# Routed feed-forward of a decoder: products over 512 tokens with transposed hidden rows, routing placed beside the groups, the loop over the chosen rows placed inside the last group

## What is computed

```python
xf = layernorm(x).reshape(-1, dim)                 # 4096 x 512
scores = softmax(xf @ w_gate.T)                    # 4096 x 8
s = (scores + expert_bias).reshape(N, 4, 2)
keep = the two groups of experts with the largest sums
topk_idx = top 2 of the kept experts               # 4096 x 2, values 0..7
weights = scores at topk_idx
counts = bincount(topk_idx)                        # rows of each run
routed_in = xf[topk_idx.reshape(-1)] * weights     # only xf[0..7] is ever gathered
h = silu(grouped(routed_in, w1, counts)) * grouped(routed_in, w3, counts)
out = (silu(xf @ sw1.T) * (xf @ sw3.T)) @ sw2.T
out = out.at[topk_idx.reshape(-1)].add(grouped(h, w2, counts))   # only rows 0..7 receive
result = x + out
```

## Time and profile before

| | |
|---|---|
| median of 3 runs | 2175.28 us (2170.5 to 2177.55) |
| the profiled execution: its own time | 2176.23 us |
| the profiled execution: its span | 2174.5 us |
| instructions | 47396 |
| TensorE matmul busy, share of the span | 2055.2 us, 95% |
| VectorE / ScalarE / GpSimd busy | 1304.4 us, 60% / 1056.6 us, 49% / 784.0 us, 36% |

### The profile page before, as it was taken

The page is one execution under the profiler, slowest core; times in us unless marked ns, Lnnn a source line. Parts: engine busy times, 40 slices in busy tenths (PEclk is TensorE's granted clock), DMA queues, the critical chain, the costliest instruction groups (busy, mean ns, idle before and its releaser), DMA issues. The chain is left out here.

```text
span 2174.5 us, 47396 instructions
## 1 busy us (share of the span) xinstructions
PE 2055.2 (95%) x14972; PEld 1579.0 (73%) x14972; DVE 1304.4 (60%) x3836; ACT 1056.6 (49%) x2763; POOL 784.0 (36%) x1435
## 2 busy tenths in 40 slices
PE   5999999999998999999979999999999699999886
PEld 4888888888885444445467888888888588888744
DVE  4777777777766677777746565555565333333354
ACT  3777676776776444444434445454544222212134
POOL 2455445545557466565522121212121111121100
PEclk8999999999999999999989999999999899999999
DMA  5121211311243121224121121111211562222100
GB/s 181 65 100 57 104 63 56 111 56 61 104 153 133 45 68 62 72 66 152 55 89 40 41 69 49 58 60 49 69 39 40 191 211 84 75 77 82 54 1 0
DMA packets 99823, 170.98 MB, mean 79 GB/s; under 512 B 12016, under 2 KB 22256, under 8 KB 99712
## 3 DMA queue, kind: packets, MB, share of 16 engines
q1 hardware_dynamic: 99712, 169.68, 23.0%
HBM read 136.08 MB, written 33.57 MB: 78 GB/s over the span
## 5 line engine op out<-in xcount | busy, mean ns | idle before, releaser
L489 POOL TENSOR_SCALAR a_probs<-a_probs,a_rinv 128x256 f32<-128x256 f32 x512 | 237.5, 482 | 283.9 <-DVE a_rinv L790 283.9
L597 ACT ACTIVATE a_probs<-a_probs,a_negm 128x256 f32<-128x256 f32 x512 | 254.6, 502 | 116.9 <-DVE a_negm L774 116.2
L489 POOL TENSOR_SCALAR c_probs<-c_probs,c_rinv 128x256 f32<-128x256 f32 x128 | 67.1, 534 | 394.6 <-DVE c_rinv L790 394.6
L774 DVE CUSTOM_DVE_ANT_0 a_probs<-bank,a_mbias 128x256 f32<-128x256 f32 x512 | 191.7, 417 | 6.3 <-PE bank L1033 4.6
L1439 ACT ACTIVATE b_gate<-bank,b_xs 128x512 f32<-128x512 f32 x128 | 87.9, 688 | 182.0 <-PE bank L1639 162.7
L783 DVE COPY a_pT<-bank 128x512 f32<-128x512 f32 x128 | 88.3, 690 | 141.8 <-PE bank L1050 141.6
L597 ACT ACTIVATE c_probs<-c_probs,c_negm 128x256 f32<-128x256 f32 x256 | 127.4, 502 | 90.0 <-DVE c_negm L774 90.0
L1050 PE MATMUL bank<-a_ident,a_probs 128*128 128x128 f32 x1024 | 155.9, 275 | 14.0 <-POOL a_probs L489 7.1
L1050 PEld LDWEIGHTS bank<-a_ident,a_probs 128*128 128x128 f32 x1024 | 122.6, 142 | 31.6 <-issue 10.4
L1639 PE MATMUL bank<-b_wg,b_xqT 128*128 128x512 bf16 x512 | 133.1, 383 | 2.3 <-DVE b_wu L1492 1.6
L1546 DVE SCALAR_TENSOR_TENSOR b_hid<-bank,b_xs,b_gate 128x512 f32<-128x512 f32 x128 | 95.9, 750 | 64.6 <-PE bank L1639 32.7
(11 more groups left out here) (289 smaller groups left out, 4786.6 us busy)
## 6 DMA issues: line engine op xcount, KB each, us to landing
m_ew<-in_L_ffn_w_dram SPq DMA_DIRECT2D x24, 512.0 KB, 8.4
a_cbuf<-in_ctx_dram SPq DMA_DIRECT2D x16, 512.0 KB, 6.9
a_xbuf<-in_x_dram SPq DMA_DIRECT2D x16, 512.0 KB, 6.4
a_resb<-in_x_dram SPq DMA_DIRECT2D x16, 512.0 KB, 3.6
x<-a_resb SPq DMA_DIRECT2D x16, 512.0 KB, 2.8
b_xbuf<-x SPq DMA_DIRECT2D x32, 256.0 KB, 2.7
b_resb<-x SPq DMA_DIRECT2D x32, 256.0 KB, 2.7
x<-b_resb SPq DMA_DIRECT2D x32, 256.0 KB, 2.0
```

What stands on the lines that cost most here:

```text
L489: last = nc.gpsimd.tensor_scalar(pr, pr, rinv[:, s, r:r + 1], 0.0, ALU.mult, ALU.add)
L597: nc.scalar.activation(pr, pr, ACT.Exp, bias=negm[:, s, h % 2, t:t + 1], scale=-1.0, accum_out=ssum[:, s, QT * (h % 2) + t:QT * (h % 2) + ...
L774: nc.vector.tensor_tensor_reduce(out=probs[:, s, h % 2, t], in0=s_bank[h][:, t * SEQ:(t + 1) * SEQ], in1=mbias[:, el.par], scale=-sm_scale ...
```

## The change

`routed_ffn_phase` is written anew; tensors are placed by hand in SBUF, and the eight banks of PSUM are shared by name. What it does:

1. 8 groups of 512 tokens take the place of 32 tiles of 128. In `gate` and `up` the weights are now the stationary operand and 512 tokens of turned rows the moving one, so the hidden rows come out already transposed, 128 features at a time. `turn_h` is gone. Each piece of hidden rows is split by ScalarE (HI, `hi_h`) and GpSimd (LO, `lo_h`), from SBUF.
2. `down` of group g stands in group g+1, one of its four tiles behind each `up`.
3. The logits are made transposed, with fp32r products of 512 columns (4 with HI and LO of the gate weights side by side, 4 more with LO of the rows), copied, and turned by 4 small transposes.
4. The routing is done per group (`route`), on VectorE, between `hidden` and `rows_out` of feature block 1 and `hidden` of feature block 2; ScalarE's Exp stands beside Silu in each group. What needs all counts (`runs`) stands behind group 6.
5. The table is made in two halves (w1 behind group 0, w3 behind group 1), with four experts side by side in strips of 32 columns, from expert weights that are loaded in two passes.
6. The loop over chosen rows has 16 steps of 512 rows. Its steps stand in "slots" between the halves (6 matmuls) of the last group's products. The scaled rows are split: GpSimd makes HI (`rows_hi`), VectorE makes LO (`rows_lo`), and `add_up` is one fp32r product of 512 columns (HI and LO side by side).
7. There is no second block and no barrier between stages.

The core of the diff (the `iteration` with `gate` and `slot` is TensorE's, the one that begins with `lo_x` VectorE's; `rows_lo` is VectorE's, `rows_hi` and `lo_h` are GpSimd's):

```diff
-                        def turn_h(el):
-                            pe.wait_ge(h_done, el.n + 1)
-                            wait_for(pe, th_lo, el.n)
-                            turn(th_bank, hid[:, el.par], th_done)
...
+        def gate(g, f, ks):
+            if ks[0] == 0:
+                if f == 0:
+                    pe.wait_ge(tx_lo, g.n * TILES + TILES)
+                wait_for(pe, silu_done, g.n * KC + f)
+            product(g_bank, lambda a, b, k: (sw[0][:, b, k, f * P:(f + 1) * P], xnT[:, g.par, a, k]), ks, g_done)
...
+    LOOP_FROM = 4
+    END_TURN, END_DOWN, END_FOLD = 23, 25, 28
+    def last_order():
+        units = [(u, f) for f in range(KC) for u in ("gate", "up", "down before")] + [("down", t) for t in range(TILES)]
+        halves = [(u, f, half) for u, f in units for half in range(2)]
+        for i, (u, f, half) in enumerate(halves):
+            yield u, f, half
+            if LOOP_FROM - 2 <= i < LOOP_FROM + STEPS + 2:
+                yield "slot", i - LOOP_FROM, 0
+            if i in (END_TURN, END_DOWN, END_FOLD):
+                yield "end", (END_TURN, END_DOWN, END_FOLD).index(i), 0
...
+        def iteration(g):
+            every = range(KC)
+            if number(g) == LAST:
...
+                        if is_step(i - 2):
+                            add_up(i - 2)
+                        if is_step(i + 1):
+                            turn_onehot(i + 1)
+                        if is_step(i):
+                            pick(i)
...
+            for f in range(KC):
+                gate(g, f, every)
+                if f == 0:
+                    turn_x(g.plus(1))
+                elif f == 1:
+                    logits_turned(g.plus(1))
+                up(g, f, every)
+                if f == 1:
+                    logits(g.plus(1))
+                if has_before(g):
+                    down(g.plus(-1), f, every)
+            if number(g) in (0, 1):
+                expert_rows(number(g))
...
+            for t in range(TILES):
+                lo_x(g.plus(1), t)
+            for f in range(KC):
+                hidden(g, f)
+                if has_before(g):
+                    rows_out(g.plus(-1), f)
+                if f == 0 and g.has(2):
+                    row_stats(g.plus(2))
+                if f == 1:
+                    route(g.plus(1))
...
+        def rows_lo(i):
+            for j in range(4):
+                dve.wait_ge(hrow_hi, 4 * i + j + 1)
+                V.scalar_tensor_tensor(hrow[:, i % 2, j, HID:2 * HID], act_a[:, i % 2, j],
+                                       weight[:, 2 * i + j // 2, j % 2:j % 2 + 1], hrow[:, i % 2, j, 0:HID].bitcast(F32),
+                                       ALU.mult, ALU.subtract).then_inc(hrow_lo, 1)
...
+        def rows_hi(i):
+            wait_for(pool, sum_done, i - 1)
+            for j in range(4):
+                wait_apart(pool, asilu_done, 4 * i + j + 1)
+                nc.gpsimd.tensor_scalar(hrow[:, i % 2, j, 0:HID], act_a[:, i % 2, j],
+                                        weight[:, 2 * i + j // 2, j % 2:j % 2 + 1], 0.0, ALU.mult, ALU.add).then_inc(hrow_hi, 1)
+        def lo_h(g, f):
+            wait_apart(pool, h_hi, g.n * KC + f + 1)
+            nc.gpsimd.tensor_tensor(hidT[:, g.par, LO, f], hid[:, f % 2], hidT[:, g.par, HI, f].bitcast(F32),
+                                    ALU.subtract).then_inc(h_lo, 1)
```

More of the change, by code:

```diff
@@ L1697, in ternary_ffn_phase, with routed_ffn_phase @@
     return phase
-def routed_ffn_phase(nc, tag, x_in, out, w_gate, w1, w2, w3, sw1, sw2, sw3, expert_bias, spent=(), tiles=TOK // P):
+def routed_ffn_phase(nc, ctx, banks, tag, x_in, out, w_gate, w1, w2, w3, sw1, sw2, sw3, expert_bias, tiles=TOK // P):
     EXPERTS, HID = w1.shape[0], w1.shape[2]
@@ new lines, in routed_ffn_phase, with sb, sem, row_of_smalls @@
+    TILES = 4
+    WIDE = TILES * P
+    groups = tiles // TILES
+    LAST = groups - 1
+    STEPS = tiles // 2
+    def sb(name, at, shape, dt=F32):
+        return nc.alloc_sbuf_tensor_at(f"{tag}_{name}", shape, dt, offset=SB_BASE + at)
+    sems = []
+    def sem(name):
+        sems.append(ctx.enter_context(nc.semaphore(f"{tag}_{name}")))
+        return sems[-1]
+    def row_of_smalls(start):
+        at = [start]
+        def small(name, shape, dt=F32):
+            here = at[0]
+            at[0] += (math.prod(shape[1:]) * 4 + 31) // 32 * 32
+            return sb(name, here, shape, dt)
+        return small
@@ new lines, in routed_ffn_phase @@
+    choice, marked, picked = [rest(n, tc) for n in ("choice", "marked", "picked")]
+    past = sb("past", 192 * KB, [P, tiles, 2, EXPERTS])
+    small = row_of_smalls(198 * KB)
+    ident = small("ident", [P, P])
+    ones = small("ones", [P, P])
+    first_out = small("first_out", [EXPERTS, DIM])
+    gateT = small("gateT", [P, KC, 2, 32], F32R)
+    xT_first = small("xT_first", [P, KC, 40])
+    table = small("table", [P, HID], F32R)
+    factor = small("factor", [P, HID])
+    pair_no = small("pair_no", [P, P])
@@ new lines, in routed_ffn_phase @@
+    pair, weight, row, run, position = [small(n, [P, tiles, 2]) for n in ("pair", "weight", "row", "run", "position")]
+    lower_e, before = [small(n, [P, EXPERTS, EXPERTS]) for n in ("lower_e", "before")]
+    counts = small("counts", [P, groups, EXPERTS])
+    csum, run_start, run_end, fold, bias_row, expert_no = [
+        small(n, [P, EXPERTS]) for n in ("csum", "run_start", "run_end", "fold", "bias_row", "expert_no")]
+    top, total, inverse = [small(n, [P, TILES]) for n in ("top", "total", "inverse")]
@@ new lines, in routed_ffn_phase, with number, before_last, has_before @@
+    r_loaded, stored = (r_loaded0, r_loaded1), (stored0, stored1)
+    first = [Element(0, n, groups) for n in range(3)]
+    last = Element(LAST // 2, LAST % 2, groups)
+    turns = [(n, k) for n in range(3) for k in range(KC)]
+    CONSTS = 9
+    def number(g):
+        return g.n if isinstance(g.n, int) else None
+    def before_last(g):
+        return number(g) == LAST - 1
+    def has_before(g):
+        return number(g) != 0
+    LOOP_FROM = 4
+    END_TURN, END_DOWN, END_FOLD = 23, 25, 28
@@ L2462, in _ @@
             clear_semaphores(nc, a.sems + b.sems + c.sems)
-    routed_ffn_phase(nc, "m", x3, out_rows, m_gate, m_w1, m_w2, m_w3, m_sw1, m_sw2, m_sw3, m_bias)
+    with ExitStack() as ctx:
+        banks = [ctx.enter_context(nc.psum_tensor(f"m_bank{i}", [P, 512], F32)) for i in range(8)]
+        m = routed_ffn_phase(nc, ctx, banks, "m", x3, out_rows, m_gate, m_w1, m_w2, m_w3, m_sw1, m_sw2, m_sw3, m_bias)
+        with nc.Block() as block:
+            @block.sync
+            def _(sp):
+                m.sync(sp)
+            @block.gpsimd
+            def _(pool):
+                m.gpsimd(pool)
+            @block.scalar
+            def _(act):
+                m.scalar(act)
+            @block.vector
+            def _(dve):
+                m.vector(dve)
+            @block.tensor
+            def _(pe):
+                m.tensor(pe)
 INPUTS = ["x", "ctx_1024", "mask_Bx1x1xS2_if1", "mask_BxS2_bk0", "L0_xattn_Wv", "L0_xattn_bv", "L0_xattn_Wk",
```

1129 lines of the change are left out of this document (559 added, 570 removed).

## The result

| | before | changed |
|---|---|---|
| device time, median (us) | 2176.4 (2170.5 to 2177.6, 4 runs) | 2092.3 (2087.3 to 2096.2, 4 runs) |
| span of the profiled execution (us) | 2174.5 | 2091.6 |
| mean granted clock of TensorE | 0.98 | 0.98 |

The ratio is 0.9617, with a 95% interval of 0.959 to 0.9645: 84 us less, where I had said 55. The time lies at the lowest edge of the range, inside it by 0.3 us, which is less than the runs differ among themselves; that it is inside at all is luck. A second measurement of the same kernel, made beside e6, e9 and e10, gave 0.9622 (0.961 to 0.9634), a median of 2093.1 us; the experiments are compared with that one.

What follows compares the result with a forecast made beforehand. TensorE was taken to bound stage 1, and barrier, table and mutual waits stage 2. Terms summed to -55.3 us on the 2174.5 span, giving 2119.2 and a forecast time of 2120 us, range 2092 to 2152.

Steps and rivals of the forecast that it cites:

- What bounds: Routed phase: TensorE bounds stage 1; stage 2, 116 us, is bound by barrier, table and a loop of mutual waits.
- Transposes and logits: Per tile and group on TensorE: hidden transposes go, -11.5 us; logits made transposed, net -7.6 us.
- Products: 1152 matmuls before and after at 0.237 us each: 0; the wait ending stage 1 goes, -1.4 us.
- Start: Before the first `gate`: +4.5 us (0 to 12); uncovered work in group 0: +4 us (0 to 12).
- Routing: Beside the groups: a route takes 11.0 us against 9.7 allowed, TensorE waits 1.3 in six groups, +8 us (0 to 30).
- Table and counting: Table of 128 records of 256 columns: +6.9 us in place of 30; counting product's wait: +1.2 us.
- The loop: Slots inside the last group: TensorE's own added work is 1.85 us per slot, 16 times, +29.6 us.
- port term: Last group's slots: VectorE and GpSimd hinder each other at SBUF, slot 4.2 us instead of 3.27, +15 us.
- The end: After the loop: transposes, w2 and fold +4.7 us, waits of TensorE +4.1, last `rows_out` and store +3.3.
- rival 1: Last group's slots and routing: ports cost nothing, slot 3.27 us, R near 9, -15 - 6, 2099 us; chance 0.24.
- rival 3: Last group's slots: in-order queues stop steps interleaving, slot 5.9 us, +27, 2147 us; chance 0.10.
- Rival 4: Routing between `hidden` 1 and 2: R is 20.5 us, TensorE waits 10.8 in seven groups, 76 not 8, 2188 us; chance 0.05.

Runs made afterwards that it cites:

- e6: Kernel before, with the transposes of x two tiles on moved from behind `up` to directly behind those of hidden: 1.0008 of the kernel before.
- e9: Changed kernel with gate weights first in SP's queue, `route` behind block 2, the end's two parts at 24 and 27: 2086.7 us, 0.959.
- e10: Changed kernel plus a probe running VectorE and GpSimd instructions together, then alone: a pair takes 0.55 us at 256 columns, 3.93 at 2048.
- e3: Changed kernel with the ranks of the experts worked out twice in each route: 2103.8 us, 0.9668 of the kernel before.
- e1: Changed kernel without VectorE's LO halves of the chosen rows (8 of 256 columns written): 2086.5 us, 0.9593 of the kernel before.
- e5: Changed kernel with all slots and the end placed after the last group's products instead of between them: 2116.5 us, 0.9734.

## Why the prediction was right or wrong

The direction held, and so did most of the mechanism; the size missed by 28 us, in four of the terms. By the steps, in the order of the prediction:

*What bounds.* Right. Stage 2 was in large part waits; TensorE is now busy 49.3 of 50 us in the loop.

*Transposes and logits.* Right: 2.24 per group for logits and their transposes, where I had 2.25. That 64 stationary columns cost the same as 128 showed too (four matmuls in 0.92).

*Products.* Wrong by some 9 us. The step that failed is "0.237 each with either operand stationary: 0". 0.237 was 2.84 to 2.87 / 12 from trains that all come behind transposes or logits, and it has 0.12 to 0.15 us of entry in it. In the kernel before each of the 96 trains pays that (96 x 0.13 = 12); now nine of the twelve trains of a group follow one another, at 2.72 / 12 = 0.227 each, and three still pay an entry (2.83 to 2.87). That makes 33.0 us of products per group where I had 34.1. The transposes cost more than I had (16 in 1.67, not 1.42), so the net against my own 37.8 is 0.86 per group.

*Start.* Counted from the last attention train (1699.51 before, 1701.36 after), the first `gate` comes 32.1 and 37.8 us later: 5.7 more, where I had 7 (the +4.5 of this term, and 2.5 of turning and logits that other terms count). Group 0 has one wait of 2.7 for `hidden`, behind which the granted clock was 0.68 for 4.2 us (below), 1.4 more: 4.1, where I had 4. But stage 1 of before (1731.64 to 2058.4, 326.8) has 4.9 us above 32 tiles of 10.06, and I left them in the sum without asking what became of them: with the 4 that made 8.9 above group 0's plain work, and it took 6.0 (35.92 from 1739.17 to 1775.09, less 96 x 0.237, 1.42, 2.25 and 3.5).

*Routing.* Wrong by 8. The step that failed is R, the length of a route: it is 8.92 us (1874.36 to 1883.28), not 11.0. The small instructions go by every 0.08 to 0.10, not 0.14, which took about 1 off, and waits against register values (0.7 in the sum) cost nothing that the rows show. The 2 for GpSimd's normalising were right: beside its four instructions there are four of VectorE of 0.48 to 0.62 instead of 0.16 to 0.21. Group 6 shows it the other way round: GpSimd normalises nothing there, the same four instructions take at most 0.19, and R is 7.07 (1985.18 to 1992.25). These rows are VectorE's, beside GpSimd's normalising:

```profile
1877.16 0.21 DVE L2127 TENSOR_TENSOR m_group_first<-m_gscore 128x12 f32<-128x12 f32 x1
1877.29 0.60 DVE L2128 TENSOR_TENSOR m_group_first<-m_gscore 128x12 f32<-128x12 f32 x1
1877.81 0.16 DVE L2127 TENSOR_TENSOR m_group_first<-m_gscore 128x8 f32<-128x8 f32 x1
```

With R under the limit, now about 9.3 (8.92 and the 0.34 to spare; four products are 10.9, not 11.4), nothing waits. The rule for the deadline was right, as e3 shows, and it was missed by very little: 2 us of R were worth 8 us of forecast.

*Table and counting.* Right: 3.92 + 3.60 where I had 6.9, and 1.4 (a wait of 1.0 in it) where I had 1.2.

*The loop.* TensorE's own part was right, 1.83 per slot for 1.85. The port term was wrong: 15 us, at most 2.7 by e1. The step that failed is the choice "between 3.27 and 4.85 I take 4.2". By the text's own figures, 0.12 beside the other in each of eight instructions, the slot was 4.85 - 0.96 = 3.9 and not 4.2. And the 0.12 was taken from a row with 2048 columns as if it were all that an instruction of 256 has to give; rows 6 held the rest. GpSimd takes 0.48 at 256 columns and 1.97 at 2048, so 1.49 / 1792 = 0.83 ns per column and 0.27 us without columns. If only the columns have to be apart, and e10 shows that it is nearly so, a pair takes 0.48 + 0.21 = 0.69 or less. I took 0.6 for it before the experiments; e10 has 0.55 without dependences, and e5 shows 3.11 per slot, just below TensorE. The Trainium skill ("SBUF — State Buffer", Who interferes with whom) says whole instructions exclude each other; e10 agrees at 2048 columns (96% of the sum) and differs at 256 (three quarters), and the measurement decides.

*The end.* 2.1 and 1.7 of waits where I had 4.1, w2 in 3.57 and the fold in 0.95 where I had 4.7 together: right.

*Rivals.* The time is closest to rival 1, but its reason ("the ports cost nothing") is not what happened: each HI takes 0.2 us longer, and the pair ends its 3.11 just 0.08 us under TensorE's 3.19, so that nearly all of it is hidden. What I had set against rival 3, the one-hots made ahead, was right: with three buffers the slot is 4.30. Rival 4 was decided by R, which came out at 9 and not 20.

Taken together. From the first `gate` to the end of the span the kernel before takes 442.9 us. My terms without the start change that by -59.8, and 2.5 of what they count stands ahead of the first `gate`: 380.6. It is 352.4 (1739.17 to 2091.6), 28.2 less:

- Group 0 and what was carried: 3 less.
- Groups 1 to 6: 225.5 (1775.09 to 2000.62) where the terms give 238.3. Routing is 8 of the 12.8, products and entries 6 x 0.86 = 5.
- The last group and the end: 91.0 (2000.62 to 2091.6) where they give 103.4, 12.4 less. The port term gives 12.3 and the cheaper products 192 x 0.01 = 1.9; so about 1.8 went the other way. The first slots and the entries at the end are longer than 0.237 per product; how the 1.8 divides among them is not worked out.

The first `gate` came 1.3 less late than I had, and the phases ahead took 1.85 longer in this profile, which makes the 27.6 between the forecast's span of 2119.2 and 2091.6. The misses in the port, the routing, the products and the start all point the same way. Only the width of the range kept the time inside it.

## What to carry to other kernels

Before a contention is priced from a long instruction, split its duration into a fixed part and a part per column, from two sizes of the same form; here only the second was excluded. Instructions that are short for other reasons then share well (a quarter of the sum passes at 256 columns, 4% at 2048); that is no reason to cut long ones up, since eight pairs of 256 columns take 4.4 us and one of 2048 takes 3.9. Where a new order puts work under a deadline, write down the deadline and the length with their uncertainty, since 0.4 us of room and 1.3 us of waiting in every group differ by 2 us of VectorE's time. And take a matmul's price from trains as they will stand after the change, not from trains that each pay an entry.
